# Cross-attention queries of a decoder layer: seven block products in place of eight, with the sums of products on VectorE

## The chip, the core and the metric

The kernel runs on one core of a Trainium2 chip. The metric is the device time of one execution in microseconds (us), as the median of several runs; lower is better. Beside the times there is one profiled execution, from which all rows below are taken.

## The reference

One decoder layer on 8 sequences of 128 tokens, model width 512, all in float32: self-attention with 32 heads of 16, cross-attention with 32 query heads and 8 key/value heads of 128 each, then a feed-forward part with a router; each of the three is added to its input and normalised. The change touches the cross-attention, of which this is the core:

```python
q = (query @ wq).reshape(bs, sq, N_Q_HEADS, D_K).transpose((0, 2, 1, 3))
k = (key @ wk).reshape(bs, sk, N_KV_HEADS, 1, D_K)          # each key head serves 4 query heads
v = (value @ wv).reshape(bs, sk, N_KV_HEADS, 1, D_V)
q = _apply_rope(q, curr_seq_pos)                             # x * cos + rotate_half(x) * sin
k = _apply_rope(k, curr_seq_pos)
raw = jnp.einsum('bhqd,bhkd->bhqk', q, k) / scale
attn = jax.nn.softmax(raw + mask, axis=-1)
out = jnp.einsum('bhqk,bhkd->bhqd', attn, v)
return out.transpose((0, 2, 1, 3)).reshape(bs, sq, N_Q_HEADS * D_V) @ wo
```

So q is a product of 1024 tokens by 512 inputs with 512 by 4096 weights.

## The kernel before

Float32 products are made of three passes: each operand is held as a "hi" and a "lo" part (hi rounded by a copy on ScalarE, lo the difference, made on VectorE or GpSimd), and `product` issues the matmuls hi·hi, hi·lo and lo·hi. Four classes follow one another: `ProjectSelf`, `AttendSelf`, `AttendCross`, `FeedForward`. Every engine has a program of its own, written out in a fixed order, and they meet only at semaphores. An engine runs its list strictly in order, so an instruction that waits holds up everything behind it on that engine.

`AttendCross` runs 64 steps n (8 groups of 4 query heads with one key/value head, times 8 sequences; `NS` = 64), each for one group and one sequence, in a pipeline:

- TensorE in step n: `transpose` (the probabilities of step n-2, 4 instructions), `scores` of step n (4 matmuls of 128x128, printed as 8), `outputs` (the product with wo for step n-3, 12 matmuls), `values` (the product with v for step n-2, 3 matmuls), `queries`: one tile of queries (one head, 4 sequences; `project`, 4 chunks of 128 inputs by 3 passes = 12 matmuls of 128x512). Tile n+5 is projected in step n, so the 64 tiles are spread one to a step. Two banks (`pj`) take the tiles in turn.
- VectorE in step n (`vector`): `inverse` (the reciprocals of the sums of step n-1), `rotate` (three instructions that read the tile's bank and write `t1`, `t2`), `turned_lo` (lo part of the transposed probabilities of step n-2, C_pT), `minima` (four pairs, the row minima that the exponentials take), the addition of the output to the row x, `output_lo` (lo part of C_o).
- ScalarE in step n: hi part of C_pT, hi part of C_o (waits for `values` of the same step), then the four exponentials of step n, then the hi part of one 128x512 piece of weights (`next_piece_hi`).
- GpSimd in step n: `C_prob` times the reciprocals of step n-1, `tile_sum` (t1 + t2 = a tile of queries), lo part of that piece of weights.
- Two score banks and two banks for the transposed probabilities alternate. Keys and values come from device memory in one transfer of 1.5 MB for a group.

The weights go through a ring of five staging slots; for each group four pieces of wq and four of wo. `FeedForward` begins its weights' split at step 57, and steps 59 and on hold some of its matmuls.

The order around the change is written out by hand in `tensor`, `vector`, `scalar` and `gpsimd` of `AttendCross`. The two lines on which TensorE meets VectorE in `values` are

```python
eng.wait_ge(self.s_phi, m + 1)
eng.wait_ge(self.s_plo, m + 1)      # turned_lo of this step, on VectorE
```

Of the kernel before, what the change touches and what calls it, by code (L numbers as in the profile page):

```python
# [456 lines left out]
class AttendSelf:  # L457
# [475 lines left out]
class AttendCross:  # L933
# [43 lines left out]

    def query(self, r):

        return by_batch(self.q[r // self.Q % 2][:, r % self.Q, :])  # L980

    def split(self, n):


        piece = 2 * self.Q * (n // B + 1) + n % B - 1
        return piece if 2 * self.Q <= piece < self.PIECES else None

    def target(self, i):

        g, j = i // (2 * self.Q), i % (2 * self.Q)  # L990
        return [t[:, :] for t in (self.w[j] if j < self.Q else self.wo[g % 2][j - self.Q])]


    def load_piece(self, eng, i):

        src = self.dram["wq" if i % (2 * self.Q) < self.Q else "wo"][i // (2 * self.Q), :, i % self.Q, :]
        self.ring.load(eng, self.first + i, src)

    def load_kv(self, eng, g):

        wait(eng, self.s_pv, B * (g - 1))
        eng.dma_start(self.kv[g % 2][:, :].bitcast(F32), self.kv_d[g]).then_inc(self.s_kv[g % 2], 16)
# [857 lines left out]
```

## Time and profile before

| | us |
|---|---|
| median of 3 runs | 877.95 (876.73 to 881.77) |
| the profiled execution, its own time | 878.4 |
| its span in the trace | 876.3 |
| TensorE (PE) matmuls busy | 854.1 (97%) |
| VectorE (DVE) busy | 604.9 (69%) |
| GpSimd (POOL) busy | 454.9 (52%) |
| ScalarE (ACT) busy | 426.1 (49%) |

"Busy" of PE is the time in which a matmul is recorded as under way; matmuls overlap each other by some 0.17 us, so rates are read from start to start. PEld is the load of weights, which lies beside the matmuls. The span is 2.1 us shorter than the execution's own time. Engines other than PE have idle time before their instructions; in the timeline it stands in square brackets with what ended it.

### The profile page before, as it was taken

How to read it: one execution, taken by the hardware profiler on the slowest of the kernel's cores; microseconds unless marked ns; L12 is line 12 of the kernel's file. 1: busy time of each engine (PE TensorE's matmuls, PEld its weight loads, DVE VectorE, ACT ScalarE, POOL GpSimd, SP SyncE). 2: the span in 40 equal slices, each digit the busy share in tenths (PEclk: the TensorE clock that was granted, in tenths of full speed). 3: DMA queues.
4: the chain of work that ended last, by engine and by line, in shares of the span. 5: the costliest groups of instructions: out<-in, count | busy, mean ns of one | idle time of the engine just before them, and what ended most of it. 6: DMA issues, size and time to landing. Idle time of an engine off the chain costs nothing.

```text
span 876.3 us, 15306 instructions
## 1 busy us (share of the span) xinstructions
PE 854.1 (97%) x4748; PEld 711.5 (81%) x4748; DVE 604.9 (69%) x2030; ACT 426.1 (49%) x1424; POOL 454.9 (52%) x406
## 2 busy tenths in 40 slices
PE   7999999999999999999999999999999999999996
PEld 6788888788877788888888888888888887778884
DVE  5466888788876776766666667667666667546646
ACT  5336977877853444444444444444444555440320
POOL 4626866766674544444444444444444569455002
PEclk9999999999999999999999999999999999999998
DMA  8679898876762111212113113122120122000001
GB/s 288 259 227 221 216 204 166 175 157 150 199 216 110 49 37 42 103 33 101 36 37 109 37 37 109 37 63 83 37 108 28 58 72 86 22 16 25 25 2 47
DMA packets 68368, 88.23 MB, mean 101 GB/s; under 512 B 7232, under 2 KB 44352, under 8 KB 67264
## 3 DMA queue, kind: packets, MB, share of 16 engines
q1 hardware_dynamic: 68288, 87.26, 35.2%
q8 instruction: 39, 0.64, 0.3%
q14 instruction: 41, 0.34, 0.2%
HBM read 64.13 MB, written 23.07 MB: 100 GB/s over the span
## 4 chain that ended last, share of the span: by engine, by line
PE 85%; DVE 6%; issue 3%; POOL 3%; ACT 2%; DMA 0%; POOLq 0%; DVEq 0%; ACTq 0%
PE banks L35 68%; PE banks L1116 6%; PE banks L1098 3%; PE banks L752 2%; PE banks L770 1%; PE banks L743 1%; DVE B_prob L840 1%; ACT B_prob L681 1%; POOL B_wv L171 1%; PE banks L367 1%; POOL x L114 0%; PE banks L122 0%; POOL D_up L171 0%; PE banks L370 0%; PE banks L371 0%
## 5 line engine op out<-in xcount | busy, mean ns | idle before, releaser
L35 PE MATMUL banks<-C_wo,C_o 128*128 128x512 f32 x768 | 192.3, 399 | 0.7 <-issue 0.5
L35 PE MATMUL banks<-xT,C_w 128*128 128x512 f32 x768 | 185.7, 390 | 0.8 <-DVE xT L137 0.8
L35 PEld LDWEIGHTS banks<-xT,C_w 128*128 128x128 f32 x768 | 143.6, 188 | 31.1 <-issue 1.6
L35 PEld LDWEIGHTS banks<-C_wo,C_o 128*128 128x128 f32 x768 | 139.6, 188 | 28.9 <-issue 1.3
L1057 ACT ACTIVATE C_o<-banks 128x512 fp32r<-128x512 f32 x64 | 38.3, 598 | 227.7 <-PE banks L35 227.7
L681 ACT ACTIVATE B_prob<-B_prob,B_top 128x128 f32<-128x128 f32 x256 | 99.6, 392 | 27.5 <-DVE B_top L840 27.5
L1037 ACT ACTIVATE C_prob<-C_prob,C_top 128x128 f32<-128x128 f32 x256 | 99.1, 391 | 10.2 <-DVE C_top L1182 10.2
L171 POOL TENSOR_TENSOR C_wo<-stage,C_wo 128x512 fp32r<-128x512 f32 x32 | 40.9, 1277 | 110.6 <-ACT C_wo L166 110.6
L171 POOL TENSOR_TENSOR C_w<-stage,C_w 128x512 fp32r<-128x512 f32 x32 | 40.9, 1278 | 101.9 <-ACT C_w L166 101.8
L1244 POOL TENSOR_TENSOR C_q<-C_t,C_t 128x512 f32<-128x512 f32 x64 | 82.9, 1296 | 16.1 <-DVE C_t L1169 16.1
L593 POOL TENSOR_TENSOR B_prob<-B_prob,B_rden 128x512 f32<-128x512 f32 x64 | 67.7, 1058 | 38.4 <-DVE B_rden L849 38.3
L1205 DVE TENSOR_TENSOR C_o<-banks,C_o 128x512 fp32r<-128x512 f32 x64 | 44.3, 692 | 41.6 <-ACT C_o L1057 41.6
L1251 POOL TENSOR_TENSOR C_prob<-C_prob,C_rden 128x512 f32<-128x512 f32 x64 | 66.6, 1040 | 10.7 <-DVE C_rden L1192 10.7
L840 DVE CUSTOM_DVE_ANT_0 B_prob<-banks,causal 128x128 f32<-128x128 f32 x256 | 58.9, 286 | 14.6 <-issue 13.4
L1116 PE MATMUL banks<-C_kv,C_q 128*128 128x128 f32 x512 | 67.6, 275 | 0.0
L1230 DVE TENSOR_TENSOR x<-banks,x 128x512 f32<-128x512 f32 x64 | 44.3, 691 | 27.0 <-PE banks L35 27.0
L1116 PEld LDWEIGHTS banks<-C_kv,C_q 128*128 128x128 f32 x512 | 62.4, 192 | 0.2
L1167 DVE TENSOR_TENSOR C_t<-banks,trig 128x512 f32<-128x512 f32 x64 | 44.2, 691 | 24.3 <-PE banks L35 24.3
L1182 DVE CUSTOM_DVE_ANT_0 C_prob<-banks,C_mask 128x128 f32<-128x128 f32 x256 | 58.9, 287 | 0.6 <-issue 0.5
L35 PE MATMUL banks<-C_pT,C_kv 128*128 128x512 f32 x192 | 54.5, 392 | 2.6 <-issue 2.4
L1048 ACT ACTIVATE C_pT<-banks 128x512 fp32r<-128x512 f32 x64 | 38.1, 596 | 30.7 <-PE banks L1098 30.7
L35 PE MATMUL banks<-cT,B_wk 128*128 128x512 f32 x192 | 52.2, 407 | 0.4 <-DVE B_t L906 0.4
(150 smaller groups left out, 1639.2 us busy)
## 6 DMA issues: line engine op xcount, KB each, us to landing
C_kv<-cross_kv_d SPq DMA_DIRECT2D x8, 1536.0 KB, 7.0
cross_kv_d<-B_v_out SPq DMA_DIRECT2D x16, 512.0 KB, 4.0
stage<-wq_dram SPq DMA_DIRECT2D x32, 256.0 KB, 2.6
stage<-wo_dram SPq DMA_DIRECT2D x32, 256.0 KB, 2.6
heads_q<-heads_q_d SPq DMA_DIRECT2D x96, 64.0 KB, 3.6
heads_k<-heads_k_d SPq DMA_DIRECT2D x96, 64.0 KB, 3.8
heads_q_d<-cT SPq DMA_DIRECT2D x8, 512.0 KB, 2.9
heads_k_d<-cT SPq DMA_DIRECT2D x8, 512.0 KB, 2.8
```

The source lines that it names most:

```text
L35: mm = eng.matmul(out, stationary[i], moving[j], start=first and n == 0, stop=last and n == len(PASSES) - 1)
L171: eng.tensor_tensor(out, self.stage[:, self.slot(n), :], hi.bitcast(F32), ALU.subtract).then_inc(self.s_lo, 1)
L593: eng.tensor_tensor(e, e, self.rden[:, m % 2, :].unsqueeze(2).broadcast_to([P, HG, S]), ALU.mult).then_inc(self.s_norm, 1)
L681: last = eng.activation(e, e, ACT.Exp, bias=self.top[:, n % 4, h:h + 1], scale=-1.0, accum_out=self.total[:, n % 2, h:h + 1])
L840: last = eng.tensor_tensor_reduce(self.prob[:, n % 4, h * S:(h + 1) * S], self.sc[n % 2][:, h * S:(h + 1) * S], self.heads.causal, 1.0, 3e ...
L1037: last = eng.activation(e, e, ACT.Exp, bias=self.top[:, n % 2, h:h + 1], scale=-1.0, accum_out=self.total[:, n % 2, h:h + 1])
L1116: mm = eng.matmul(self.sc[n % 2][:, h * S:(h + 1) * S], self.q[s // 4][:, h, tok], keys, start=True, stop=True)
L1182: last = eng.tensor_tensor_reduce(self.prob[:, n % 2, h * S:(h + 1) * S], self.sc[n % 2][:, h * S:(h + 1) * S], self.mask[:, n % B, :], 1. ...
L1205: eng.tensor_tensor(self.o[1][:, :], self.ov, self.o[0][:, :].bitcast(F32), ALU.subtract).then_inc(self.s_olo, 1)
L1230: eng.tensor_tensor(row, self.yb, row, ALU.add).then_inc(self.s_add, 1)
L1244: eng.tensor_tensor(self.query(r), by_batch(t1), by_batch(t2), ALU.add).then_inc(self.s_sum, 1)
L1251: eng.tensor_tensor(e, e, self.rden[:, (n - 1) % 2, :].unsqueeze(2).broadcast_to([P, self.Q, S]), ALU.mult).then_inc(self.s_norm, 1)
```

## The change

The first 16 tiles of queries (groups 0 and 1) are projected as before, but two to a step from step 3 on. The other 48 tiles are made in 12 "pairs". A pair k is two heads by the 8 sequences, that is four tiles; it is a 2 by 2 block product (inner halves of 256, tokens in two halves), done with seven block products instead of eight (Winograd's form). A block product is two chunks by three passes, 6 matmuls. A pair takes four steps, n = 7+4k to 10+4k, here called its phases 0 to 3:

- TensorE: phase 0 products 0 and 1 (12 matmuls), phase 1 product 2 and half of 3 (9), phase 2 the other half and product 4 (9), phase 3 products 5 and 6 (12). They go to four banks, alpha, beta, gamma and delta (1, 5, 6, 7); two of those were the second score bank and the second bank for transposed probabilities, so scores and transposed probabilities now have one bank each.
- VectorE: `add_products` and `tile_from_products` add the products: seven additions of 128x512 for a pair. Three of the four tiles are summed in their bank and rotated there; the fourth is summed into C_h in SBUF and rotated from there. Before a pair can begin, `token_sums` forms the sums and differences of the tokens once, in steps 3 to 8: 16 instructions of 128x512, and eight lo parts, all from SBUF to SBUF.
- ScalarE: one copy of a bank for a pair (p1), and the hi parts of the seven blocks of weights (128x256 each) in place of two pieces.
- GpSimd: four sums of 128x256 of the weights (`blocks_lo`, phase 1 of preparing a pair), and seven lo parts of 128x256 in place of two of 128x512.
- Keys and values are loaded for each step by itself (196 KB, five buffers), stored in device memory in another layout; wo pieces are split in phases 0 and 1; the first feed-forward pieces are split from step 55 on instead of 57.

The core of the diff:

```diff
     def queries(self, eng, n):
 
-        if n + self.PRE + 1 < self.TILES:
-            self.project(eng, n + self.PRE + 1)
+        if n < self.AT:
+            self.project(eng, 2 * n + 2)
+            self.project(eng, 2 * n + 3)
+        k, phase = self.multiplying(n)
+        if k is None:
+            return
...
+        if phase == 0:
+            wait(eng, self.s_e, k)
+            self.block_product(eng, k, 0, self.alpha, x(0, 0), (True, True))
+            self.rotated(eng, k - 1, 0)
+            self.block_product(eng, k, 1, self.beta, x(0, 1), (True, True))
...
+        if phase == 3:
...
+            eng.wait_ge(self.s_p5, k + 1)
+            self.block_product(eng, k, 5, self.delta, x(1, 1), (True, True))
+            eng.wait_ge(self.s_h2, k + 1)
+            self.block_product(eng, k, 6, self.gamma, t(4), (True, True))
...
+    def add_products(self, eng, n):
...
+        if phase == 1:
...
+            eng.tensor_tensor(self.e[:, :], self.alpha, self.p1[:, :], ALU.add).then_inc(self.s_e, 1)
+        if phase == 2:
...
+            eng.tensor_tensor(self.p5[:, :], self.delta, self.e[:, :], ALU.add).then_inc(self.s_p5, 1)
+            eng.wait_ge(self.s_st, 7 * k + 5)
+            eng.tensor_tensor(self.e[:, :], self.gamma, self.e[:, :], ALU.add).then_inc(self.s_h1, 1)
...
+            eng.tensor_tensor(self.h[:, :], self.gamma, self.p5[:, :], ALU.add).then_inc(self.s_h2, 1)
+
+    def tile_from_products(self, eng, r):
...
+        k, i = self.pair(r)
+        if i == 3:
+            eng.wait_ge(self.s_h2, k + 1)
+            return self.h[:, :]
+        eng.wait_ge(self.s_st, 7 * k + (2, 7, 6)[i])
...
+        bank = (self.beta, self.gamma, self.delta)[i]
+        eng.tensor_tensor(bank, bank, (self.p1, self.e, self.p5)[i][:, :], ALU.add)\
+           .then_inc(self.s_u, 1)
+        eng.wait_ge(self.s_u, 3 * k + i + 1)
+        return bank
...
     def vector(self, eng, n):
 
         self.inverse(eng, n - 1)
-        if n + self.PRE < self.TILES:
-            self.rotate(eng, n + self.PRE)
+        self.add_products(eng, n - 1)
+        tiles = self.tiles(n)
+        for r in tiles[:1]:
+            self.rotate(eng, r)
         self.turned_lo(eng, n - 2)
         self.minima(eng, n)
...
         self.output_lo(eng, n - 2)
+        for r in tiles[1:]:
+            self.rotate(eng, r)
+        self.token_sums(eng, n)
...
-            wait(eng, self.s_top, n - 1)
+            eng.wait_ge(self.s_kv[n % self.SLOTS], 16 * (n // self.SLOTS + 1))
+            wait(eng, self.s_top, n)
...
+        if phase == 1:
...
+            eng.tensor_tensor(S1, b[:, 0:256], b[:, 256:512], ALU.add).then_inc(self.s_raw, 1)
+            eng.wait_ge(self.s_raw, 4 * k + 1)
+            eng.tensor_tensor(S2, S1, a[:, 0:256], ALU.subtract).then_inc(self.s_raw, 1)
+            eng.tensor_tensor(S3, a[:, 0:256], b[:, 0:256], ALU.subtract).then_inc(self.s_raw, 1)
...
+            eng.tensor_tensor(S4, a[:, 256:512], S2, ALU.subtract).then_inc(self.s_raw, 1)
...
-    SPLIT = {57: (0, 1), 58: (2, 3), 59: (4, 5), 60: (6, 7), 61: (8, 9), 62: (10, 11), 63: (12,)}
+    SPLIT = {55: (0, 1), 56: (2, 3), 57: (4, 5), 58: (6, 7), 59: (8, 9), 60: (10, 11), 61: (12,)}
```

On VectorE, before, the list of every step of the cross-attention begins like this (C_t_139 and C_t_138 are t1 and t2, C_pT_136 the lo part of the transposed probabilities, L1180 opens the minima):

```order
L1192 RECIPROCAL C_rden<-C_total 128x4 [waits C_norm,C_exp]
L1167 TENSOR_TENSOR C_t_139<-banks,trig 128x512 [waits C_sum,C_pj]
L1168 TENSOR_TENSOR C_t_138<-banks,trig 64x512
L1169 TENSOR_TENSOR C_t_138<-banks,trig 64x512
L1198 TENSOR_TENSOR C_pT_136<-banks,C_pT_135 128x512 [waits C_phi]
L1180 MEMSET C_carrier 128x1 [waits C_exp,C_tp,C_sc]
```

Now, in a step of phase 3 (C_p_169 is p5, C_p_167 is p1):

```order
L1496 RECIPROCAL C_rden<-C_total 128x4 [waits C_norm,C_exp]
L1408 TENSOR_TENSOR C_p_169<-banks,C_e 128x512 [waits C_st,C_e]
L1410 TENSOR_TENSOR C_e<-banks,C_e 128x512 [waits C_st]
L1415 TENSOR_TENSOR C_h<-banks,C_p_169 128x512 [waits C_p5,C_sin,C_cos]
L1432 TENSOR_TENSOR banks<-banks,C_p_167 128x512 [waits C_p1,C_st]
L1385 TENSOR_TENSOR C_t_182<-banks,trig 128x512 [waits C_sum,C_u]
L1390 TENSOR_TENSOR C_t_181<-banks,trig 64x512
L1391 TENSOR_TENSOR C_t_181<-banks,trig 64x512
L1502 TENSOR_TENSOR C_pT_179<-banks,C_pT_178 128x512 [waits C_phi]
```

Between the reciprocals and the lo part of C_pT there stand seven instructions where there were three. In a step of phase 2 the list is

```order
L1496 RECIPROCAL C_rden<-C_total 128x4 [waits C_norm,C_exp]
L1404 TENSOR_TENSOR C_e<-banks,C_p_167 128x512 [waits C_u,C_h2,C_st,C_p1]
L1385 TENSOR_TENSOR C_t_182<-C_h,trig 128x512 [waits C_sum,C_h2]
L1390 TENSOR_TENSOR C_t_181<-C_h,trig 64x512
L1391 TENSOR_TENSOR C_t_181<-C_h,trig 64x512
L1502 TENSOR_TENSOR C_pT_179<-banks,C_pT_178 128x512 [waits C_phi]
```

Four stand there, three of which read C_h and trig, both in SBUF. In phases 0 and 1 there are four as well: one addition into a bank and the three of the rotation.

On GpSimd, now, the end of a step of phase 1 and the beginning of phase 2 (C_block_sum are the sums of weight blocks, C_wo_127 a lo part, C_prob the probabilities):

```order
L1589 TENSOR_TENSOR C_block_sum_153<-stage 128x256 [waits ring_piece3,ring_piece4,C_pj,C_st]
L1591 TENSOR_TENSOR C_block_sum_152<-C_block_sum_153,stage 128x256 [waits C_raw]
L1592 TENSOR_TENSOR C_block_sum_154<-stage 128x256
L1594 TENSOR_TENSOR C_block_sum_155<-stage,C_block_sum_152 128x256 [waits C_raw]
L171 TENSOR_TENSOR C_wo_127<-stage,C_wo_126 128x512 [waits ring_hi]
L1563 TENSOR_TENSOR C_prob<-C_prob,C_rden 128x512 [waits C_rden]
L1556 TENSOR_TENSOR C_q_134<-C_t_182,C_t_181 128x512 [waits C_sin,C_cos]
```

The last three stood in this order before too; the four sums ahead of them are new.

## Rows read from the trace of the kernel before

**Rows 1.** The page: busy time of the engines, and TensorE's clock by slice.
```profile
PE 854.1 (97%) x4748; PEld 711.5 (81%) x4748; DVE 604.9 (69%) x2030; ACT 426.1 (49%) x1424; POOL 454.9 (52%) x406
PEclk9999999999999999999999999999999999999998
```

**Rows 2.** Busy time by window, steps 4 to 59: PE, PEld, DVE, ACT, POOL, clock, DMA.
```profile
294.00:713.00 419.00, 419.00 (x2181) 355.14 (x2180) 290.27 (x897) 183.54 (x619) 203.58 (x172) 1.00 0.18 60
```

**Rows 3.** Timeline of one step: start us, us, engine, line, operation, count [idle].
```profile
485.22 0.84 PE L35 MATMUL banks<-C_pT,C_kv 128*128 128x512 f32 x3
...
485.90 2.89 PE L35 MATMUL banks<-xT,C_w 128*128 128x512 f32 x12
486.10 0.60 ACT L1057 ACTIVATE C_o<-banks 128x512 fp32r<-128x512 f32 x1 [3.73 <-PE banks L35]
...
486.73 0.69 DVE L1205 TENSOR_TENSOR C_o<-banks,C_o 128x512 fp32r<-128x512 f32 x1 [0.62 <-ACT C_o L1057]
...
488.26 0.18 DVE L1192 RECIPROCAL C_rden<-C_total 128x4 f32<-128x4 f32 x1 [0.84 <-ACT C_prob L1037]
...
488.62 0.60 PE L1098 MATMUL banks<-ident,C_prob 128*128 128x128 f32 x4
488.82 0.69 DVE L1167 TENSOR_TENSOR C_t<-banks,trig 128x512 f32<-128x512 f32 x1 [0.38 <-PE banks L35]
488.83 1.27 POOL L171 TENSOR_TENSOR C_wo<-stage,C_wo 128x512 fp32r<-128x512 f32 x1 [3.94 <-ACT C_wo L166]
...
489.87 3.02 PE L35 MATMUL banks<-C_wo,C_o 128*128 128x512 f32 x12
490.07 1.03 POOL L1251 TENSOR_TENSOR C_prob<-C_prob,C_rden 128x512 f32<-128x512 f32 x1
...
490.97 0.69 DVE L1198 TENSOR_TENSOR C_pT<-banks,C_pT 128x512 fp32r<-128x512 f32 x1
...
492.73 0.39 PE L35 MATMUL banks<-C_pT,C_kv 128*128 128x512 f32 x1
```

**Rows 4.** Timeline of step 3, where two tiles were rotated in a row.
```profile
287.18 0.18 DVE L1192 RECIPROCAL C_rden<-C_total 128x4 f32<-128x4 f32 x1
287.28 0.66 DVE L1167 TENSOR_TENSOR C_t<-banks,trig 128x512 f32<-128x512 f32 x1
...
287.97 0.69 DVE L1168 TENSOR_TENSOR C_t<-banks,trig 64x512 f32<-64x512 f32 x1
...
288.68 0.68 DVE L1169 TENSOR_TENSOR C_t<-banks,trig 64x512 f32<-64x512 f32 x1
289.39 0.69 DVE L1198 TENSOR_TENSOR C_pT<-banks,C_pT 128x512 fp32r<-128x512 f32 x1
...
290.19 0.93 PE L35 MATMUL banks<-C_pT,C_kv 128*128 128x512 f32 x3 [1.95 <-issue]
```

**Rows 5.** Timeline of VectorE in the feed-forward part: instructions without a wait between them.
```profile
756.36 0.68 DVE L1571 TENSOR_TENSOR D_sq<-banks,D_pos 128x512 f32<-128x512 f32 x1
756.95 0.68 DVE L1578 TENSOR_TENSOR D_hT<-D_sq,D_hT 128x512 fp32r<-128x512 f32 x1
```

**Rows 6.** Timeline of the feed-forward part: GpSimd and VectorE at once.
```profile
769.46 1.35 POOL L171 TENSOR_TENSOR D_down<-stage,D_down 128x512 fp32r<-128x512 f32 x1 [1.37 <-ACT D_down L166]
769.93 1.43 DVE L1578 TENSOR_TENSOR D_hT<-D_sq,D_hT 128x512 fp32r<-128x512 f32 x1 [0.27 <-ACT D_hT L1378]
```

**Rows 7.** All instructions of line 1578, 755 to 790 us: shortest/median/longest ns.
```profile
L1578 DVE TENSOR_TENSOR D_hT<-D_sq,D_hT x8: 681/683/1426, 757.0 to 784.6; 128x512 fp32r<-128x512 f32 x8
```

**Rows 8.** Timeline of TensorE behind the last tile of queries.
```profile
717.62 0.84 PE L35 MATMUL banks<-C_pT,C_kv 128*128 128x512 f32 x3
718.31 0.60 PE L1098 MATMUL banks<-ident,C_prob 128*128 128x128 f32 x4
...
723.21 0.94 PE L35 MATMUL banks<-C_pT,C_kv 128*128 128x512 f32 x3 [0.30 <-issue]
```

More of the change, by code:

```diff
@@ L576, in sync @@
                     eng.wait_ge(self.s_vout[i], 16 * B // 2)
-                self.cross.load_kv(eng, 0)
+                for i in range(self.cross.SLOTS):
+                    self.cross.load_kv(eng, i)
             if n == self.NS + 4:
@@ L976, in live, with pair @@
         return 0 <= n - lag < self.NS
+    def pair(self, r):
+        return divmod(r - self.PLAIN, 4)
     def query(self, r):
[L980 to L986, printed above, removed]
-    def target(self, i):
-        g, j = i // (2 * self.Q), i % (2 * self.Q)
-        return [t[:, :] for t in (self.w[j] if j < self.Q else self.wo[g % 2][j - self.Q])]
@@ L994, in load_piece @@
-    def load_piece(self, eng, i):
[L996 to L1002, printed above, removed]
+        half, j = r // self.Q, r % self.Q
+        if r >= self.PLAIN:
+            k, i = self.pair(r)
+            half, j = 2 * (k // 2 + 2) + i // 2, 2 * (k % 2) + i % 2
@@ new lines, in splits, with block, raw_block @@
+    def splits(self, n):
+        if n in self.SPLIT:
+            return self.SPLIT[n]
+        k, phase = self.preparing(n)
+        return (12 + 4 * k + phase,) if k is not None and phase < 2 else ()
+    def target(self, i):
+        kind, g, j = self.ORDER[i]
+        return [t[:, :] for t in (self.w[j] if kind == "wq" else self.wo[g % 2][j])]
+    def block(self, k, i, lo):
+        return self.blocks[(7 * k + i) % len(self.blocks)][:, lo, :, :]
+    def raw_block(self, k, i):
+        return self.block_sums[(7 * k + i) % len(self.blocks)][:, 1, :]
@@ new lines, in staged, with wait_staged, T_part @@
+    def staged(self, k, second):
+        n = self.first + 14 + 4 * k + second
+        return self.ring.stage[:, self.ring.slot(n), :], n
+    def wait_staged(self, eng, k):
+        for second in range(2):
+            n = self.staged(k, second)[1]
+            eng.wait_ge(self.ring.s_piece[self.ring.slot(n)], 16 * (n // self.ring.SLOTS + 1))
+    def T_part(self, i, lo, c):
+        if i == 3:
+            return self.rows.xT[:, 4:8, lo, c, :]
+        return by_batch(self.T[i][:, lo, c, :])
@@ new lines, in T_sum, with done_at, load_kv @@
+    def T_sum(self, i, c):
+        return self.T_sums[3][:, 4:8, 1, c, :] if i == 3 else by_batch(self.T_sums[i][:, 1, c, :])
+    def load_piece(self, eng, i):
+        kind, g, j = self.ORDER[i]
+        self.ring.load(eng, self.first + i, self.dram[kind][g, :, j, :])
+    def done_at(self, i):
+        if i < 12:
+            return next((n for n in self.SPLIT if i in self.SPLIT[n]), 0)
+        k, j = divmod(i - 12, 4)
+        return self.AT - 4 + 4 * k + j
+    def load_kv(self, eng, i):
+        wait(eng, self.s_pv, i - self.SLOTS + 1)
+        eng.dma_start(self.kv[i % self.SLOTS][:, :].bitcast(F32), self.kv_d[i // B][:, i % B, :])\
+           .then_inc(self.s_kv[i % self.SLOTS], 16)
@@ L1161, in rotate @@
     def rotate(self, eng, r):
[L1163 to L1169 removed]
+        t1 = self.t1[:, r % 2, :]
@@ L1242, in tile_sum @@
         eng.wait_ge(self.s_sin, r + 1)
+        if r == 2 * self.Q:
+            for i in range(2):
+                eng.wait_ge(self.before.s_vout[i], 16 * B)
         t1, t2 = self.t1[:, r % 2, :], self.t2[:, r % 2, :]
```

330 lines of the change are left out of this document (271 added, 59 removed).

## The prediction

> **What bounds the kernel now.** I read the page first. Its first section shows PE busy for 97% of the span, VectorE for 69%, GpSimd and ScalarE for about half, and the clock row stays at its top level [rows 1]. An average over stages says little, so next came the busy times by window: in the 419 us that hold steps 4 to 59 of the cross-attention PE has matmuls under way for all 419.00 us, at a granted clock of 1.00, with VectorE busy 290 us (69%) and GpSimd 204 us [rows 2]. That is 419.0 / 56 = 7.48 us a step, and nothing but matmuls is in it. So a matmul taken away from these steps is worth its full time, as long as nobody else becomes late.
>
> Who would be late is read from the timeline of one step [rows 3]. I count from S, the start of `values` on PE (485.22; the next is at 492.73, 7.51 later). The 12 matmuls of `queries` fill 485.90 to 488.62, so one is 2.72 / 12 = 0.227 us. From S the other engines run one chain: the last matmul of `values` ends, ScalarE copies C_o (S+0.88), does the four exponentials, VectorE's reciprocals start at S+3.04, its rotation follows, and the lo part of C_pT starts at S+5.75, because the rotation had to wait for PE until S+3.60. `values` needs that lo part at S+7.51. Thus VectorE is the second limit, with a chain that goes through every step.
>
> The trace shows what happens when that chain is longer. In step 3 six instructions of two rotations ran one after the other, the C_pT part started at 289.39, and PE stood idle for 1.95 us until `values` began at 290.19, 0.80 after that start [rows 4]. The same rows give the pitches: reciprocals to next instruction 0.10, between instructions of a rotation 0.69 to 0.71. Two instructions with no wait between them have a pitch of 0.59 [rows 5]; I take 0.60 for such a sum and 0.72 for one whose successor waits for its result.
>
> **What goes.** 12 pairs, 42 matmuls in place of 48: 72 x 0.227 = -16.3 us. It is 1.36 us a pair. The 12 matmuls of an ordinary step become 12, 9, 9, 12, so between `values` and `values` PE alone would need 7.49 us when 12 lie between, and 7.49 - 3 x 0.227 = 6.81 when 9 do.
>
> **The seven additions, phase 3.** The chain from S to the next `values` is 3.04 + 0.10 + the instructions ahead of C_pT + 0.80. In phase 3 these are p5, e and h (3 x 0.60), the sum in the bank (0.72, since the rotation waits for it) and the rotation (0.72 + 0.70 + 0.71): 4.65. The chain is 8.59, and PE, with the 9 matmuls of phase 2 in between, would need 6.81: a wait of 1.8 us. This happens 12 times: +21.6 us. Nothing hides it, since PE's next instruction is the waiting one, and behind it stand the products 5 and 6 that VectorE waits for next. No row shows VectorE writing to a bank; the nearest are its reads of one, 0.69. With all pitches at 0.71 the wait is 2.3, with all at 0.60 it is 1.3; 12 times that is 16 to 28 us. I take 1.8, from the two pitches that rows show.
>
> In phases 0 and 1 four instructions take 0.72 + 2.13 = 2.85, and the chain is 6.79 against 7.49 for PE (phase 0 starts only when product 6 is done, at S+3.60 as in the rows: 3.60 + 2.85 + 0.80 = 7.25). No wait, with 0.2 us to spare in phase 0. In phase 2 e and the rotation take 0.60 + 2.13 and the chain is 6.67 against 6.81: just covered, if nothing is added.
>
> **The rotation of C_h, phase 2.** Something is added. Its three instructions read both inputs from SBUF. In the steps before, every 128x512 instruction of VectorE has one input in a bank. Where both are in SBUF, the row of the feed-forward part shows 1.43 us in place of 0.68: it began at 769.93 while GpSimd was in an instruction from 769.46 to 770.81, and it ended 0.55 after that one [rows 6]. Seven others of that line had medians of 683 ns, the longest is the 1426 ns of another such meeting [rows 7]. In phase 2 GpSimd makes the lo part of a wo piece from S+3.61 to S+4.88, and then the 1.03 us on C_prob [rows 3], in an order that the change leaves as it is. The first instruction on C_h starts at S+3.74, so it meets the first and ends at about 4.88 + 0.55 = 5.43; the C_prob one gets in next, until 6.40, and the second on C_h ends at 6.95; the third at 7.65. `values` then starts at about S+8.48 instead of 6.81: 1.7 us. 11 times before step 55: +18.7 us. Its bounds are 0 (the two engines don't meet) and 2.3 (three meetings); GpSimd's four new sums, 0.65 to 1.27 each (half of a 128x512 one, or all of it), may push its lo part later, which moves the meeting but doesn't remove it. I take 1.7.
>
> The Trainium skill, page "SBUF — State Buffer", section "Who interferes with whom", states the rule that speaks against this change: a VectorE instruction with two SBUF inputs and a GpSimd one that reads SBUF exclude each other for a whole instruction, whichever began first, while one with at most one SBUF input is free. The trace agrees, by the 1.43 against 0.68. By that rule phase 2 costs the sum above; without it the time would be the first rival's.
>
> **The beginning, steps 3 to 9.** Two tiles a step are the same matmuls, only earlier (24 of them, 10.2 us a step), so neutral in themselves. But the second rotation stands at the end of VectorE's step: C_o's lo part starts at S+1.51, three instructions of rotation then end at S+4.25, and PE wants its bank at S+0.68+2.72 = 3.40: 0.95 us, in steps 4, 5 and 6, +2.9. `token_sums` puts 24 instructions of 0.65 there, all from SBUF to SBUF, six in step 7. Step 7's second rotation ends at S+4.25, its six end near S+8.2, and ScalarE's hi parts of those sums hold back its copy of C_pT in step 8; its lo part and 0.80 bring `values` to about S+10, against 7.49: 2.5, and one or two meetings with GpSimd make it 3.5. Bounds: 1 and 9 us for all of these that I put at 3.5. Together +6.4.
>
> **The end, steps 55 to 59.** These lose the queries of tiles 60 to 63 that moved forward, and would be 4.77 us on PE (7.49 - 2.72); the rows of such a step show the next transposes 0.69 behind `values`, with nothing between, and the next `values` 5.59 later, with waits of its own [rows 8]. VectorE still rotates the last three tiles: step 56 has a chain of 6.79 (+2.0), step 57 one of 6.06 (+1.3) and the meeting (+1.7). Feed-forward pieces split two steps earlier give GpSimd room in steps 62 to 64: -1. Together +4.0.
>
> **Taken at nothing.** ScalarE: the block copies and p1 stand behind the exponentials, and its busy time is 184 of 419 us [rows 2]; the copy of C_pT it delays has until S+6. GpSimd: 204 of 419 us, per pair some 5 us more; C_prob has a whole step. One score bank: `scores` waits for the minima of the step before, which end 4 us ahead; also in a stalled phase they precede it. Transposed probabilities: `values` already waited for the same copies. SP: small transfers of keys and values are issued three steps ahead, a piece's load waits for GpSimd's lo part behind which nothing urgent stands; if one were late it would be seen as a wait of `scores` on DMA. Stores of keys in 512-byte pieces lie in the first third, where PE doesn't wait for transfers.
>
> **Sum.** -16.3 + 21.6 + 18.7 + 6.4 + 4.0 = +34.4. Against the profiled execution's own 878.4 that is 912.8, 913. That execution stands 0.4 us above the median of 877.95, which changes nothing.
>
> **Rivals.**
> 1. VectorE and GpSimd don't meet, or hardly. For it: in 419 us of the old steps no VectorE instruction was lengthened. Against: none had two inputs in SBUF. Then -18.7, -1.7 and -1 (beginning) fall away: 891.
> 2. The cover holds and the kernel gets faster. Mechanism: VectorE begins its additions earlier than its reciprocals let it, or does them at a pitch so short that C_pT's lo part is ready. Place: phase 3. The cover is complete if the seven take 6.81 - 3.94 = 2.87 us, 0.41 each; then -16.3, +5.4 for the beginning and +2.3 for the end (both without meetings) remain: 870. The point from which it decides is a wait of 8.6 / 12 = 0.7 us in phase 3: with less, and no meeting, the kernel isn't slower. Against it stand the reciprocals, which wait for the exponentials and stand first in the list, and the 1.95 us of step 3 with six instructions.
> 3. GpSimd becomes the limit as well: blocked by VectorE in turn, its sums and lo parts come late, product 0 and C_prob with them, and the tail gets longer. Some 1.5 us a pair more: 931. For it: 7 + 4 new instructions a pair. Against: 204 us and 12 x 5 of 450 is a busy share of about 60%.
> 4. The seven products are not really fewer matmuls: the list of PE has 6 per product and 42 a pair, so no.
>
> **Chances.** Forecast (both waits) 0.58, its own range 902 to 924. Rival 1 and partial meetings, 886 to 902: 0.24. Rival 3, over 924: 0.08. Rival 2 with what lies between it and rival 1: 0.10, of which 0.05 is faster by more than 0.5% (below 873.6), 0.03 within 0.5%, 0.02 just slower. 0.5%, 4.4 us, is about what a measurement of this kernel can tell from no change. So faster 0.05, same 0.03, slower 0.92. The range of 8 in 10, with rival 1 in it and half of rival 3: 886 to 931.
>
> **What would show it.** Right: in the timeline `values` of phase 3 preceded by about 1.8 us of idle PE, with seven VectorE instructions between reciprocals and C_pT; in phase 2 instructions on C_h of 1.2 to 1.6 us where GpSimd is busy, and about 1.7 us of idle PE; a four-step period of 7.5 + 7.5 + 8.5 + 8.6 = 32.1 us where it was 29.9; matmuls on C_block of 0.227 us. Wrong: instructions on C_h of 0.69 us throughout (rival 1), PE without gaps (rival 2), PE waiting before a product for GpSimd's lo parts or before `scores` for a transfer, or gaps in phases 0 and 1 as well.

## The result and the profile after

The changed kernel takes 918.9 us (median of 4 runs, 918.1 to 920.3), the kernel before 879.7 beside it: a ratio of 1.046, interval 1.043 to 1.049. The forecast was 913 us, in a range of 886 to 931, and slower with a chance of 0.92. The profiled execution is the slowest of the four, 920.3 us with a span of 918.5; the span of before was 876.3.

The page of the changed kernel, to be set beside [rows 1]: PE has 72 matmuls fewer and a smaller share of a longer span, and VectorE, ScalarE and GpSimd have more to do.

```profile
PE 848.9 (92%) x4676; PEld 696.9 (76%) x4676; DVE 696.3 (76%) x2138; ACT 446.4 (49%) x1504; POOL 530.9 (58%) x514
PEclk9999999999999998999999999999999999999998
```

Its busy times by window, in the columns of [rows 2], for the steps 3 to 9, 10 to 53 and 54 to 58. Before, PE had matmuls under way all the time (419.00 of 419.00 us). In the middle window it now has 320.71 us in 354.11: 33.4 us idle in 44 steps, 0.76 a step. VectorE was busy for 69%; it now is for 82% there, and for 91% in the first window.

```profile
292.19:368.21 76.02, 66.85 (x316) 53.68 (x316) 69.21 (x148) 29.86 (x95) 49.09 (x44) 0.96 0.19 59
368.21:722.32 354.11, 320.71 (x1650) 265.41 (x1651) 289.89 (x782) 157.32 (x547) 214.87 (x225) 1.00 0.18 58
722.32:753.95 31.63, 28.14 (x148) 22.98 (x148) 24.06 (x84) 18.92 (x61) 21.93 (x19) 1.00 0.34 108
```

The timeline of PE over four steps, only the rows of `values`. Their starts are called S, and S(n) for step n. In [rows 3] these rows had no bracket and stood 7.51 apart. Now the interval ahead of the first row is 7.51, then follow 8.41, 8.67 and 7.57, and the pattern repeats every 32.2 us.

```profile
479.88 0.84 PE L35 MATMUL banks<-C_pT,C_kv 128*128 128x512 f32 x3
...
488.29 0.93 PE L35 MATMUL banks<-C_pT,C_kv 128*128 128x512 f32 x3 [1.44 <-issue]
...
496.96 0.93 PE L35 MATMUL banks<-C_pT,C_kv 128*128 128x512 f32 x3 [1.60 <-issue]
...
504.53 0.84 PE L35 MATMUL banks<-C_pT,C_kv 128*128 128x512 f32 x3
```

What VectorE does ahead of the first wait (phase 2): the sum e, then the rotation of C_h. The first two instructions of the rotation take 1.61 and 1.41 us, and in the same stretch GpSimd (POOL) is in two instructions of its own. VectorE's end 0.54 us behind GpSimd's (485.32 behind 484.78, 486.76 behind 486.22), and the second of GpSimd's takes 1.49 where [rows 3] had 1.03.

```profile
482.92 0.18 DVE L1496 RECIPROCAL C_rden<-C_total 128x4 f32<-128x4 f32 x1 [0.84 <-ACT C_prob L1145]
483.10 0.69 DVE L1404 TENSOR_TENSOR C_e<-banks,C_p 128x512 f32<-128x512 f32 x1
...
483.49 1.29 POOL L171 TENSOR_TENSOR C_wo<-stage,C_wo 128x512 fp32r<-128x512 f32 x1 [0.80 <-ACT C_wo L166]
483.71 1.61 DVE L1385 TENSOR_TENSOR C_t<-C_h,trig 128x512 f32<-128x512 f32 x1
484.73 1.49 POOL L1563 TENSOR_TENSOR C_prob<-C_prob,C_rden 128x512 f32<-128x512 f32 x1
485.35 1.41 DVE L1390 TENSOR_TENSOR C_t<-C_h,trig 64x512 f32<-64x512 f32 x1
486.77 0.69 DVE L1391 TENSOR_TENSOR C_t<-C_h,trig 64x512 f32<-64x512 f32 x1
487.49 0.69 DVE L1502 TENSOR_TENSOR C_pT<-banks,C_pT 128x512 fp32r<-128x512 f32 x1
```

And ahead of the second wait (phase 3): seven instructions between the reciprocals and the lo part of C_pT (below: the C_pT part). Their starts, up to that of the C_pT part, are 0.59, 0.60, 0.60, 0.72, 0.72, 0.71 and 0.72 apart. `values` starts 0.79 behind the start of the C_pT part.

```profile
491.41 0.18 DVE L1496 RECIPROCAL C_rden<-C_total 128x4 f32<-128x4 f32 x1 [0.84 <-ACT C_prob L1145]
491.51 0.68 DVE L1408 TENSOR_TENSOR C_p<-banks,C_e 128x512 f32<-128x512 f32 x1
492.10 0.68 DVE L1410 TENSOR_TENSOR C_e<-banks,C_e 128x512 f32<-128x512 f32 x1
492.70 0.68 DVE L1415 TENSOR_TENSOR C_h<-banks,C_p 128x512 f32<-128x512 f32 x1
493.30 0.69 DVE L1432 TENSOR_TENSOR banks<-banks,C_p 128x512 f32<-128x512 f32 x1
494.02 0.69 DVE L1385 TENSOR_TENSOR C_t<-banks,trig 128x512 f32<-128x512 f32 x1
...
496.17 0.69 DVE L1502 TENSOR_TENSOR C_pT<-banks,C_pT 128x512 fp32r<-128x512 f32 x1
```

All instructions of line 1390, the second of the three of a rotation, shortest, median and longest in ns: every one of the 12 on C_h is lengthened, none of the 52 on a bank.

```profile
L1390 DVE TENSOR_TENSOR C_t<-banks,trig x52: 692/694/696, 257.8 to 734.5; 64x512 f32<-64x512 f32 x52
L1390 DVE TENSOR_TENSOR C_t<-C_h,trig x12: 1410/1411/1412, 388.8 to 740.7; 64x512 f32<-64x512 f32 x12
```

The span by stretches, in us. "Forecast" is worked out here, by setting the terms of the prediction on the starts S that the trace of before shows:

| stretch | before | forecast | after |
|---|---|---|---|
| to S(3) | 290.2 | 290.2 | 292.2 |
| S(3) to S(10) | 52.6 | 70.3 | 76.0 |
| S(10) to S(59) | 367.3 | 384.9 | 385.7 |
| S(59) to the end | 166.2 | 165.2 | 164.6 |

The 70.3 are 52.6 + 10.9 for four tiles of queries moved forward (48 x 0.227) + 6.4 + 1.8 for the wait at S(10) - 1.4 for the six matmuls that the steps 8 and 9 have fewer. In the first stretch the change alters little, namely how keys and values are stored and loaded; the profiled executions of the ten experiments below, whose kernels are equal to the changed one there, give 289.6 to 292.8, so its 2 us are within what one execution differs from another. One stretch is off by more, 5.7 us, and it is the beginning of the cross-attention.

### The profile page after: what moved, and what is told of

The parts are those of the page before. It is cut to its first block, busy times and chain, and to the rows that moved or that the text cites. A ratio compares the mean times of both kernels' runs of the same rounds, so it can differ in the third digit from the quotient of the medians.

```text
span 918.5 us, 15763 instructions
## 1 busy us (share of the span) xinstructions
PE 848.9 (92%) x4676; PEld 696.9 (76%) x4676; DVE 696.3 (76%) x2138; ACT 446.4 (49%) x1504; POOL 530.9 (58%) x514
## 4 chain that ended last, share of the span: by engine, by line
PE 80%; issue 8%; DVE 6%; ACT 3%; POOL 1%; DMA 1%; POOLq 0%; DVEq 0%; SPq 0%; ACTq 0%
PE banks L35 63%; PE banks L1273 6%; PE banks L1256 3%; PE banks L752 2%; PE banks L770 1%; PE banks L743 1%; DMA stage<-wv_dram 1%; ACT B_prob L681 1%; DVE B_prob L840 1%; PE banks L122 1%; POOL B_wv L171 1%; PE banks L367 1%; PE banks L371 0%; PE banks L370 0%; DVE B_t L905 0%
## 5 line engine op out<-in xcount | busy, mean ns | idle before, releaser
L1145 ACT ACTIVATE C_prob<-C_prob,C_top 128x128 f32<-128x128 f32 x256 | 99.0, 391 | 10.2 <-DVE C_top L1486 10.2
L35 PE MATMUL banks<-C_pT,C_kv 128*128 128x512 f32 x192 | 57.8, 409 | 45.8 <-issue 45.6
L1563 POOL TENSOR_TENSOR C_prob<-C_prob,C_rden 128x512 f32<-128x512 f32 x64 | 72.0, 1125 | 19.6 <-DVE C_rden L1496 19.6
L35 PEld LDWEIGHTS banks<-C_pT,C_kv 128*128 128x128 f32 x192 | 33.6, 190 | 64.2 <-issue 59.2
L35 PE MATMUL banks<-xT,C_block 128*128 128x512 f32 x288 | 71.5, 390 | 0.0
L1509 DVE TENSOR_TENSOR C_o<-banks,C_o 128x512 fp32r<-128x512 f32 x64 | 44.3, 692 | 28.6 <-ACT C_o L1165 28.6
L35 PEld LDWEIGHTS banks<-xT,C_block 128*128 128x128 f32 x288 | 54.1, 188 | 11.6
L35 PE MATMUL banks<-C_T,C_block 128*128 128x512 f32 x216 | 56.8, 400 | 0.0
L1612 POOL TENSOR_TENSOR C_block<-C_block_sum,C_block 128x256 fp32r<-128x256 f32 x48 | 35.2, 753 | 32.5 <-ACT C_block L1211 32.5
L35 PE MATMUL banks<-B_wv,cT 128*128 128x512 f32 x192 | 51.5, 401 | 0.6 <-POOL B_wv L171 0.5
```

The source lines that it names most:

```text
L35: mm = eng.matmul(out, stationary[i], moving[j], start=first and n == 0, stop=last and n == len(PASSES) - 1)
L1145: last = eng.activation(e, e, ACT.Exp, bias=self.top[:, n % 2, h:h + 1], scale=-1.0, accum_out=self.total[:, n % 2, h:h + 1])
L1509: eng.tensor_tensor(self.o[1][:, :], self.ov, self.o[0][:, :].bitcast(F32), ALU.subtract).then_inc(self.s_olo, 1)
L1563: eng.tensor_tensor(e, e, self.rden[:, (n - 1) % 2, :].unsqueeze(2).broadcast_to([P, self.Q, S]), ALU.mult).then_inc(self.s_norm, 1)
```

## The experiments

Ratios are to the kernel before, timed beside each experiment (medians of 878.4 to 878.7 us); they are formed from runs taken together and can differ by 0.002 from the quotient of the medians given here.

**e1: the C_pT part ahead of the rotation.** From step 10 on, VectorE makes the lo part of C_pT right behind the additions.

```
+        late = n > 9
+        if late:
+            self.turned_lo(eng, n - 2)
         for r in tiles[:1]:
             self.rotate(eng, r)
-        self.turned_lo(eng, n - 2)
+        if not late:
+            self.turned_lo(eng, n - 2)
         self.minima(eng, n)
```

> From step 10 on the lo part of C_pT stands between the additions of products and the rotation; nothing else moves and no work goes. Chain theory (PE waits only because seven, or four lengthened, VectorE instructions stand ahead of that lo part): it starts at S+4.9 in phase 3 and S+4.7 in phase 2, both before PE's S+6.8, so both waits go: 12 x 1.6 + 12 x 1.6 = -38 us, 881 (875 to 890), period 28.6 to 29.2 us. Rival (VectorE and the collisions fill the period, so the order doesn't matter): the period stays above 31.5 us, 910 or more.

Measured: 909.2 us, ratio 1.037 (1.035 to 1.039). A miss. `values` has no long bracket any more, but the period is 31.6 us, as the rival has it, and the time is within 1 us of the rival's. From the timeline of e1:

```profile
482.15 0.69 DVE L1391 TENSOR_TENSOR C_t<-C_h,trig 64x512 f32<-64x512 f32 x1
...
483.85 0.40 ACT L1145 ACTIVATE C_prob<-C_prob,C_top 128x128 f32<-128x128 f32 x1 [2.60 <-DVE C_top L1486]
483.96 1.13 PE L1273 MATMUL banks<-C_kv,C_q 128*128 128x128 f32 x8 [0.87 <-DVE C_top L1486]
...
486.63 0.57 ACT L1156 ACTIVATE C_pT<-banks 128x512 fp32r<-128x512 f32 x1
...
495.03 0.69 DVE L1502 TENSOR_TENSOR C_pT<-banks,C_pT 128x512 fp32r<-128x512 f32 x1 [1.23 <-ACT C_pT L1156]
```

The minima still stand behind the rotation. The exponentials wait for them (2.60), and so does PE's `scores` (0.87), whose only bank the minima free. ScalarE's copy of C_pT is queued behind the exponentials, and in the next step the C_pT part waits for that copy (1.23), with the rotation now behind it. I read this as a loop of VectorE and ScalarE through every step. The rival's full VectorE it isn't, for from 480 to 512 us VectorE is busy for 26.7 of 32.0. What had to move is everything that others wait for, not one instruction of it. That both the C_pT part and the minima have to move is argued from these rows; e2 tests it.

**e2: the rotation behind the C_pT part and the minima.**

```
         self.add_products(eng, n - 1)
...
-        for r in tiles[:1]:
-            self.rotate(eng, r)
+        late = n > 9
+        if not late:
+            for r in tiles[:1]:
+                self.rotate(eng, r)
         self.turned_lo(eng, n - 2)
         self.minima(eng, n)
+        if late:
+            for r in tiles[:1]:
+                self.rotate(eng, r)
```

> From step 10 on the lo part of C_pT and the minima both stand ahead of the rotation. Chain theory: as with the lo part alone, 880 (873 to 890); if the minima, which the exponentials wait for, were late there, this one is up to 5 us the faster of the two; if the late rotation makes PE wait before its bank (phase 1, half of product 3), slower by 1 us a pair. Rival (throughput): 910 or more.

Measured: 879.0 us, ratio 1.001 (1.000 to 1.003): 40 us come back with not one instruction fewer. The rows of `values` over one period of e2, which is 28.76 us, and the busy times of a stretch, where PE has 32.00 us of matmuls in 32.00:

```profile
601.16 0.84 PE L35 MATMUL banks<-C_pT,C_kv 128*128 128x512 f32 x3
...
608.66 0.84 PE L35 MATMUL banks<-C_pT,C_kv 128*128 128x512 f32 x3
...
615.47 0.84 PE L35 MATMUL banks<-C_pT,C_kv 128*128 128x512 f32 x3
...
622.43 0.84 PE L35 MATMUL banks<-C_pT,C_kv 128*128 128x512 f32 x3
...
629.92 0.84 PE L35 MATMUL banks<-C_pT,C_kv 128*128 128x512 f32 x3
```

```profile
600.00:632.00 32.00, 32.00 (x166) 27.03 (x165) 29.27 (x76) 15.57 (x55) 22.05 (x24) 1.00 0.22 68
```

The changed kernel has 28.95 of PE and 25.86 of VectorE in the same window. So VectorE's total load (29.27 of 32.00 here) was not the limit, but the chain from the reciprocals to `values`. The meetings with GpSimd are still there, only later, while PE has work (timeline of VectorE in e2):

```profile
499.11 0.86 DVE L1385 TENSOR_TENSOR C_t<-C_h,trig 128x512 f32<-128x512 f32 x1
500.00 1.66 DVE L1390 TENSOR_TENSOR C_t<-C_h,trig 64x512 f32<-64x512 f32 x1
501.68 1.44 DVE L1391 TENSOR_TENSOR C_t<-C_h,trig 64x512 f32<-64x512 f32 x1
```

Two stretches of e2 keep idle time of PE: the beginning (S(3) to S(10), 73.2 us), and the end, where S(54) to S(59) takes 31.4 us against 31.6 in the changed kernel, with PE now waiting for GpSimd's sum of a tile (1.67) and for VectorE's C_o part (1.06).

**e3: the changed kernel with its fourth tile rotated out of a bank.** The three instructions on C_h read the bank of beta, so numbers other than the tile's; nothing else differs.

```
-            return self.h[:, :]
+            return self.beta
```

> The fourth tile of each pair is rotated from the bank beta in place of C_h, so it is rotated from other numbers: the same three instructions, with one SBUF input in place of two. Collision theory: they take 0.69 us each, the wait of phase 2 (1.45) goes, and in step 57 too: 12 x 1.6 = -19 us, 900 (896 to 903), phase 3 unchanged at 1.6. Rival (the fourth tile's wait has another cause, such as C_h being ready late or the additional e): 915 to 919.

Measured: 899.7 us, ratio 1.026 (1.024 to 1.027). This is 19.2 us less than the changed kernel, against 18.7 + 1.7 in the prediction's sum. Line 1390 of e3, and `values` of phases 2 and 3 in its timeline: the first wait is gone, the second stays as it was.

```profile
L1390 DVE TENSOR_TENSOR C_t<-banks,trig x64: 692/694/695, 255.2 to 720.5; 64x512 f32<-64x512 f32 x64
```

```profile
479.28 0.86 PE L35 MATMUL banks<-C_pT,C_kv 128*128 128x512 f32 x3
...
487.89 0.93 PE L35 MATMUL banks<-C_pT,C_kv 128*128 128x512 f32 x3 [1.60 <-issue]
```

**e4: the row addition short.** The addition of the output to the row x, behind the minima, leaves out 504 of its 512 columns.

```
-            eng.tensor_tensor(row, self.yb, row, ALU.add).then_inc(self.s_add, 1)
+            eng.tensor_tensor(row[:, 0:8], self.yb[:, 0:8], row[:, 0:8], ALU.add).then_inc(self.s_add, 1)
```

> The addition of the output to the row x is done on 8 of 512 columns in each cross-attention step: 0.5 us less work for VectorE in each of 64 steps, but behind the lo part of C_pT and ahead of a wait. Chain theory: 919, at most 3 us less, from steps 3 to 8 where VectorE never waits (six steps of 0.5). Rival (VectorE's total load is what PE waits for): 0.5 x 50 = -25 us, 894.

Measured: 917.4 us, ratio 1.046 (1.044 to 1.047). 64 instructions shrink from 0.69 to 0.16 us, 34 us of VectorE's work, and 1.5 us come of it. The waits stay at 1.45 and 1.59, and S(10) to S(59) at 385.7. So VectorE's work off the chain, taken away, brings nothing from step 10 on; that added work would cost as little isn't shown.

**e5: half of the token work to GpSimd.** From here to e9 the base is e2, and the subject is its beginning: S(3) to S(10) takes 73.2 us, and PE's own work there is 62.1 (52.6 + 42 matmuls of 0.227). The "token work" are the sums x12 and x22 of steps 3 and 4 and the eight lo parts of steps 7 and 8.

```
+    def token_work(self, eng, n):
...
+            if n in (3, 4):
+                out, at = ((self.x12, 0), (self.x22, 2))[n - 3]
+                eng.tensor_tensor(by_batch(out[c][:, :]), part(1, 0, at + c), part(1, 1, at + c), ALU.add).then_inc(self.s_x, 1)
         for i in {7: (1, 2), 8: (3, 4)}.get(n, ()):
...
         for r in self.tiles(n):
             self.tile_sum(eng, r)
+        if n > 4:
+            self.token_work(eng, n)
```

> The kernel of e2 (rotation behind minima and lo part from step 10 on), and in steps 3, 4, 7 and 8 twelve of the 24 instructions on token sums go from VectorE to GpSimd (the sums x12 and x22, and the eight lo parts of T). Theory A (the beginning is bound by VectorE, whose SBUF to SBUF instructions of 1.2 to 1.8 us each met GpSimd's): the twelve gave it some 14 us of work, S(3) to S(10) falls from 73 us to about 65, and the time is 871 (869 to 875). Rival B (the beginning is bound by something else, the weight pieces or transfers): S(3) to S(10) stays at 73 and the time is 879. Rival C (GpSimd takes the twelve at 0.7 to 1.8 us each and is now late itself with its own lo parts): 880 to 884.

Measured: 879.4 us, ratio 1.001 (0.998 to 1.003). A miss: S(3) to S(10) is 72.9. The number is that of B, but no transfer or weight piece shows up as the cause: steps 3 and 4 become shorter (table below), and in step 8 PE waits 2.49 for ScalarE's copy of C_pT, in step 9 1.64 for GpSimd's C_prob.

**e6: the second rotation early.** In the steps with two tiles it stands ahead of the row addition, the C_o part and the token sums. Against e2:

```
         self.minima(eng, n)
-        if late:
-            for r in tiles[:1]:
-                self.rotate(eng, r)
+        for r in tiles if late else tiles[1:]:
+            self.rotate(eng, r)
...
         self.output_lo(eng, n - 2)
-        for r in tiles[1:]:
-            self.rotate(eng, r)
```

> The kernel of e2, and in the steps with two tiles before step 10 the second rotation stands ahead of the row addition and the token sums in place of behind them. Theory A (PE's three waits of about 0.8 us in steps 4 to 6 are for that rotation, and the rest of the beginning is VectorE's total): the three waits go, but VectorE has as much to do as before, so between 0 and 2 us less: 878. Rival B (only the order binds in the beginning, not the total): 5 us and more less, 874 or below.

Measured: 871.5 us, ratio 0.991 (0.989 to 0.994), which is the size that B gave. S(3) to S(10) falls from 73.2 to 67.3.

**e7: the edits of e5 and e6 together**, on e2.

> The edits of e5 and of e6 together on the kernel of e2. Theory: with half of the token work gone the order of the rest decides, so the three waits of about 0.8 us now count as well: 869 (867 to 873), below the 878.5 of the kernel before, ratio 0.989. Rival: the two gains overlap, and it comes out as e5 alone (871), or the beginning isn't bound by VectorE (879).

Measured: 872.8 us, ratio 0.992 (0.989 to 0.995): no better than e6 alone. The distances from S(3) to S(4) and so on tell why (us, from the timelines of PE):

| | 3-4 | 4-5 | 5-6 | 6-7 | 7-8 | 8-9 | 9-10 |
|---|---|---|---|---|---|---|---|
| changed kernel | 11.68 | 11.93 | 11.93 | 11.39 | 10.92 | 9.58 | 8.59 |
| e2 | 11.67 | 11.92 | 11.94 | 11.38 | 10.92 | 8.50 | 6.82 |
| e5 | 10.34 | 11.30 | 11.84 | 11.39 | 10.15 | 9.25 | 8.67 |
| e6 | 11.68 | 11.09 | 11.10 | 10.33 | 8.15 | 8.00 | 6.94 |
| e7 | 10.35 | 10.20 | 10.33 | 10.31 | 8.47 | 6.93 | 9.77 |

In steps 3 to 6 VectorE's order and its load bind one behind the other: either edit alone leaves 11 us and more in most steps, both together give 10.2 to 10.4, which is PE's own work. In steps 7 to 9 the lo parts on GpSimd hurt: it makes C_prob late, and PE waits for that (timeline of e7):

```profile
352.57 0.66 PE L1257 MATMUL banks<-ident,C_prob 128*128 128x128 f32 x4 [2.75 <-POOL C_prob L1576]
```

**e8: e2 and e3 together.**

> The kernel of e2 and the edit of e3 together: the fourth tile is rotated out of a bank (other numbers than those of the tile) in place of C_h. Theory (with the rotation behind the minima the meetings on C_h fall into a stretch that PE covers, PE without a gap from step 10 to 59): the instructions on C_h fall from up to 1.7 us to 0.69 and the time doesn't change: 879 (877 to 881). Rival (VectorE still binds there in some step, so the meetings still cost): at least half of what e3 gained shows again, 870 or below. Between them, 1 to 2 us for the C_h of the first steps.

Measured: 876.1 us, ratio 0.997 (0.995 to 0.999), 0.9 below the range of the theory and 6 above the rival's. What cost 19 us in the changed kernel costs 3 once PE has work beside it. The period is 28.63 in place of 28.76 us, 1.4 us over 11 periods; where the rest lies, and through what wait it gets to PE, isn't shown.

**e9: only the four sums on GpSimd.** e7 with the eight lo parts of T back on VectorE.

> The kernel of e7 with the eight lo parts of T (steps 7 and 8) back on VectorE, so that only the four sums x12 and x22 (steps 3 and 4) are on GpSimd. Theory (three limits in turn: steps 3 to 6 are VectorE's total and its order together, and there e7's 41.2 us from S(3) to S(7) are all PE; steps 7 to 9 are GpSimd's and ScalarE's once the lo parts lie there, 25.2 us in e7 against 23.1 in e6): S(3) to S(10) is 41.2 + 23.1 = 64.3 us, and the time 869.5 (868 to 871), ratio to the kernel before 0.990. Rival (it is the later steps that gain from the lo parts' leaving VectorE, and the wait in e7 is for something else): S(7) to S(10) stays at 25 or more, and the time is 872 or above.

Measured: 870.3 us, ratio 0.990 (0.988 to 0.992), the lowest median of all and 1% below the kernel before; the runs of e6 (871.5) overlap with it. S(7) to S(10) is 22.6 us (e6 23.1, e7 25.2). S(3) to S(10) is 65.2, not 64.3: in the profiled execution the 24 matmuls behind S(3) took 7.23 us in place of the 5.64 of e7, and the window over them shows a mean granted clock of 0.77 (e7: 1.00). Within it the clock is 0.50, that is 1.2 GHz, from 294.79 to 296.79. Without those 1.6 us the stretch is 63.6.

```profile
294.00:301.00 7.00, 7.00 (x27) 5.57 (x27) 5.93 (x8) 2.92 (x11) 7.00 (x6) 0.77 0.53 175
```

**e10: the changed kernel with the edit of e6 alone.**

> The changed kernel itself with only the edit of e6: in the steps with two tiles the second rotation stands behind the minima, ahead of the row addition and the token sums; from step 10 on nothing differs from the changed kernel. Theory (the order in the beginning cost what the forecast put too low, and it adds up with the waits of the later steps): 918.9 - 7 = 912 (910 to 914), S(3) to S(10) 76.0 - 6 = 70. Rival (the beginning is all VectorE's total load from its collisions with GpSimd, and e6 gained only because the later steps were free): 917 or above.

Measured: 913.7 us, ratio 1.040 (1.038 to 1.042), so 5.2 us less; S(3) to S(10) is 69.0 in place of 76.0, and from S(10) to the end both have 550.3 (the profiled execution of the changed kernel is 1.4 above its median and that of e10 0.8 below, hence 7 us by the traces and 5 by the times). Of the 7.0 us, 2.7 lie in steps 4 to 6, 2.8 in step 7 and 1.6 in step 8. So the place of three instructions is worth about as much as the forecast missed in the beginning, but not in the same steps, as the next section shows.

## Why the prediction was right, and where it was off

The prediction was right in its number and in the mechanism of both waits, which are 40 of the 51 us that it added. Of the rest, the beginning was mis-sized, and one of its waits came out at the right size by another path.

- **PE's own work, and 72 matmuls fewer.** Right. The period without waits is 28.76 in e2, against 4 x 7.49 - 1.36 = 28.6.
- **Phase 3, 1.8 us twelve times.** Right: the pitches are those of [rows 4] and [rows 5], and a sum written to a bank takes 0.69 like one that reads it, which no row of before showed. The bracket says 1.60, yet the interval is 8.67 against 8.61 in the forecast: an interval grows by some 0.26 more than its bracket (8.67 - 6.81 - 1.60), part of it because `values` behind a wait takes 0.93 for 0.84. The upper bound given for this wait was miscounted: with all seven pitches at 0.71 it is 2.1 us, 25 in all, not 2.3 and 28.
- **Phase 2, 1.7 us eleven times.** Right in size and mechanism; e3 takes it away alone. It was built on the one meeting of [rows 6]. The order foreseen (GpSimd's lo part, C_h, C_prob, C_h) is the one that the trace shows, and the third instruction on C_h runs free at 0.69, as foreseen. The Trainium skill, page "SBUF — State Buffer", section "Who interferes with whom", states that a VectorE instruction with two SBUF inputs contends with one of GpSimd that reads SBUF, and that one with at most one SBUF input doesn't, apart from modes that use both port pairs. The trace agrees: of line 1390 all 12 instructions with both inputs in SBUF take 1.41, all 52 with a bank 0.69.
- **Phases 0 and 1, and everything taken at nothing.** Right: no bracket there, and no wait of PE for a transfer or a lo part of GpSimd from step 10 on.
- **The end, +4.0.** Right as a whole, off in its parts. S(55) to S(56) takes 6.80 as forecast (4.77 + 2.0), S(56) to S(57) 6.87 against 7.77 (4.77 + 3.0), because there the first instruction on C_h ran free at 0.68, and the two steps behind them take 5.24 and 5.11 against 4.77. e2 shows that the rotation's place isn't all there is to it: its end is only 0.2 us shorter.
- **The beginning, +6.4.** This is the term that was mis-sized: it came to +12.1 (76.0 - 52.6 - 10.9 - 1.8 + 1.4), just over the 11.9 that the prediction's own upper bound allows (2.9 + 9). By steps, from one S to the next, with "PE alone" as the distance of before, 2.72 more for each tile moved there and 0.68 less where three matmuls are gone:

| steps | PE alone | measured | over | forecast |
|---|---|---|---|---|
| 3 to 6 | 41.0 | 46.9 | 5.9 | 2.9 |
| 7 | 7.5 | 10.9 | 3.4 | 3.5 |
| 8 | 6.8 | 9.6 | 2.8 | 0 |

**Steps 3 to 6.** The second rotations were about right: three waits of PE for C_t, 0.81, 0.78 and 0.79, where 0.95 each was forecast (the prediction's own S+4.25 and S+3.40 give 0.85). The sum had nothing for three more waits, before `values` of the steps 4, 5 and 6: 1.17, 0.39 and 0.36. The token sums of the step before stand ahead of the reciprocals and push the whole chain back: four of them take 6.6 us in step 3 and 4.7 in step 4, at a forecast of 2.6. The timeline of step 4:

```profile
308.21 0.69 DVE L1452 TENSOR_TENSOR C_T_sum<-C_x,C_T_sum 128x512 f32<-128x512 f32 x1
308.82 1.79 DVE L1453 TENSOR_TENSOR C_x<-xT 128x512 f32<-128x512 f32 x1
310.53 1.22 DVE L1452 TENSOR_TENSOR C_T_sum<-C_x,C_T_sum 128x512 f32<-128x512 f32 x1
311.68 1.22 DVE L1453 TENSOR_TENSOR C_x<-xT 128x512 f32<-128x512 f32 x1
312.81 0.17 DVE L1496 RECIPROCAL C_rden<-C_total 128x4 f32<-128x4 f32 x1
```

The prediction used the rule of the meeting with full weight for three instructions a pair, and only "one or two meetings" for 24 instructions of the same kind. In the trace 15 of the 24 are lengthened, to 0.98 to 1.79 us.

**Step 7.** The size was right by luck, for the path was another. The prediction let ScalarE's hi parts hold back its copy of C_pT. In the trace that copy ends at 348.45, and the C_pT part starts only at 349.29, right behind VectorE's own six token instructions: they end at S+10.2 (349.27), not at the S+8.2 of the prediction. GpSimd's lo part beside them takes 1.75 for 1.28. The timeline of step 7:

```profile
343.37 2.40 DVE L1466 TENSOR_TENSOR C_T_sum<-C_x,C_x 128x512 f32<-128x512 f32 x2
...
345.69 3.58 DVE L1472 TENSOR_TENSOR C_T<-C_T_sum,C_T 128x512 fp32r<-128x512 f32 x4
...
347.86 0.59 ACT L1156 ACTIVATE C_pT<-banks 128x512 fp32r<-128x512 f32 x1
...
349.29 0.65 DVE L1502 TENSOR_TENSOR C_pT<-banks,C_pT 128x512 fp32r<-128x512 f32 x1
...
350.04 1.62 PE L35 MATMUL banks<-C_pT,C_kv 128*128 128x512 f32 x3 [3.26 <-issue]
```

**Step 8.** Here the prediction left out what a long wait does to PE. During the wait of 3.26 us the granted clock falls, and behind it it stays at 0.50, that is 1.2 GHz, for more than 5 us. The windows around it:

```profile
346.00:350.00 4.00, 0.78 (x4) 0.32 (x2) 4.00 (x8) 2.44 (x5) 1.48 (x2) 0.87 0.20 66
350.00:352.00 2.00, 1.96 (x5) 1.60 (x6) 1.40 (x9) 0.31 (x1) 1.92 (x4) 0.50 0.00 0
...
356.00:360.00 4.00, 4.00 (x24) 3.47 (x23) 3.10 (x14) 0.60 (x1) 1.29 (x2) 1.00 0.19 66
```

There `values` takes 1.62 in place of 0.93 and nine matmuls on C_T 4.04 in place of the 2.24 of e6, where the wait is 0.48 and the clock stays up: 0.7 + 1.8 us, with the transposes 0.2 more. These 2.7 are the 2.8 of step 8. How long the low clock lasts differs from one execution to another: in e1, e2, e3, e4 and e8, which have the same wait, the nine matmuls take 2.93 to 4.04 us. So part of these 2.8 us belongs to the one profiled execution, which is 1.4 us above the median.

My first reading, that VectorE's load alone bound the beginning, fell with e5. Load, order and GpSimd bind there in turn, and e6, e7 and e10 separate them. What stays open is why e4, e8 and e9 had a lower clock in step 3, and how the last 1.5 us of the beginning in e9 (63.6 against 62.1 of PE's own work) divide.

## What to carry to other kernels

- Before a saving on the busiest engine is counted, follow the second engine's chain through one step, with every new instruction ahead of the one that is waited for. Here 72 matmuls fewer were worth 16 us (an estimate, 72 x 0.227), and the order around them cost 47: exactly the same instructions take 918.9 us in the order of the changed kernel and 871.5 in that of e6.
- When such an instruction is moved forward, move with it whatever else others wait for: the C_pT part alone (e1) left the period at 31.6 us, the C_pT part and the minima (e2) brought it to 28.8.
- Apply a rule of contention to every instruction that it covers, not only to those in the steady part. Here 24 instructions before step 9 were given one or two meetings, and 15 had one.

## What the runs showed of the hardware

- A VectorE instruction of 512 columns with both inputs in SBUF that meets one of GpSimd takes 0.86 to 1.8 us, mostly 1.2 to 1.8, where it takes 0.69 alone. GpSimd's instructions are lengthened in turn: its 128x512 lo part from 1.28 to 1.75, the one on C_prob from 1.04 to 1.49. With one input in a bank none of the 52 instructions of line 1390 was lengthened.
- Waits of PE of 1.4 to 1.6 us, two in 32 us, left the granted clock at 1.00 over 354 us. The wait of 3.26 us was followed by 0.50 in all six profiled executions that have it (the changed kernel, e1, e2, e3, e4, e8).
- Behind the wait of 1.95 us at S(3) the granted clock fell to 0.50 for 2 to 3 us in the profiled executions of e4, e8 and e9, with matmuls under way all the time; in the other nine, which have the same wait, it stayed at 1.00. What brought it isn't shown; the wait alone didn't.
